# Turning convolved rows between two queries' products, keys ahead of broadcasts, and a bias add between left-over parts

## The chip, the core and the metric

The kernel runs on one core of a Trainium2 chip. The core has a matrix engine (TensorE, PE in the profile, with its weight loads as PEld), a vector engine (VectorE, DVE), an activation engine (ScalarE, ACT), GpSimd (POOL) and SyncE (SP), which issues most DMAs. Each engine works through its own list of instructions in order and they meet only through semaphores. The metric is the device time of one execution in microseconds.

## The reference

One tower block over 64 images of 2 x 104 x 104. Cut to what matters:

```python
concat = concatenate((x, left_up, right_up, left_down, right_down), axis=1)      # 10 channels
normed = (concat - mean) * rsqrt(var + 1e-7) * gamma + beta                      # per image
h = conv(normed, W, stride 8) + b                      # 169 tokens of 128 per image
xn = layernorm(h);  q, k, v = xn @ Wqkv.T              # 8 heads of 64
qp = exp(q * scale @ proj.T);  kp = exp(k @ proj.T)
D = qp @ kp.sum(tokens);  context = kp.T @ v
h = h + (qp @ context / (D + 1e-6)) @ Wout.T + bout
h = h + moe(layernorm(h))                              # 8 experts, the best 2, silu(x W) * (x V) @ W2
```

The attention is over all tokens of one image. The convolution's share that comes from `beta` is the same in all images; it is computed once as the map `cbeta`.

## The kernel before

The kernel has a token stage (to about 706 us of the trace) and an expert stage behind it. The change lies in the token stage.

The token stage goes over 32 pairs of images, in groups of four pairs (8 images). A step works on three pairs at once, as a pipeline: in step n, pair n is convolved and normalised (`a`), pair n-1 gets its queries, keys and context (`b`), pair n-2 its division by D and its attention output (`c`), and pair n-3 its routing (`d`). k is n modulo 4. While a group is worked on, the patches of the next group are made in seven front pieces: TensorE transposes a piece into bank 0 and VectorE multiplies it by gamma (L745). `TURN` says where: k = 1 and 2 have pieces at the places `front(2)` and `front(3)`, k = 3 at `front(0)`, `front(1)` and `front(2)`, k = 0 has none. The last group makes no pieces. In k = 1 VectorE also computes the image shift of the next group (L703, L707) right behind the bias add. Three steps more (n = 32 to 34) empty the pipeline.

The order on each engine is written out by hand in its `step`. The parts that the change and the prediction touch:

- TensorE: `q_feature(j)` (three matmuls of 362 columns, L627 to L629, into bank 4 or 5), for j = 0, 1 at the step's start; the sums D (L528); the convolution (L535, ten matmul instructions into bank 1); `q_feature(2)` and `(3)`; the transposes of the convolved rows h1 (L548, bank 2); `front(0)`; `broadcast(0)` and `(1)` (L498), which spread 1/D of two heads over the partitions, into banks 7 and 1 in turn; `k_tokens(0)` and `(1)` (three matmuls of 512 columns, L627 to L629, banks 4 and 5); `broadcast(2)`, `k_tokens(2)`, `broadcast(3)`; the first part of the context (L640); the transposes of the normalised rows (L633); `front(1)`; the products of queries and context (L581, bank 7); the rest of the context (L640, L646); `front(2)`; the transposes of the updated rows (L609); L653; `front(3)`.
- VectorE: 1/D (L812), whose value is split for TensorE's float32r input into a high part, four copies (L824), and a left-over part, four subtractions (L830), one for each of two images and two halves of their tokens; `rden_ready` is counted up behind the last. Then the bias add `h1 = conv + cbeta` (L837, two instructions), which waits for `conv_done` and releases `h1_ready`; statistics of the h1 transposes (L751, L754); `normalise(0)` and `(1)` (L794: the query features times a broadcast, each waits for its broadcast); in k = 3 the first front piece; `xtok` (L855), the normalised rows, which waits for `rstd` from GpSimd (L1128, L1130); `normalise(2)` and `(3)`; the choice of experts; and so on.
- ScalarE: the exponents of the four query products (L1066, L1067; `q_exp`) and of the three key products (L1083; `k_exp`), which also free banks 4 and 5.

## Time and profile before

| | |
|---|---|
| median of three runs | 1203.25 us (1201.57 to 1204.62) |
| the profiled execution's own time | 1201.72 us |
| its span, first to last instruction | 1199.9 us |
| granted TensorE clock, mean over the span | 0.968 of full speed |
| busy: PE, PEld | 1095.0 us (91%), 926.2 us (77%) |
| busy: DVE, ACT, POOL | 858.7 us (72%), 567.8 us (47%), 605.2 us (50%) |

Busy time is summed over the whole span and hides which wait ends last in a stage; matmuls are pipelined, so their recorded durations overlap and the distance from one start to the next says more. The steps themselves are very alike: between 95 and 645 us, the starts of two convolutions are 19.1 to 20.2 us apart, with the same spacing at every k. In the timeline, instructions of one line that follow each other closely are merged into one row (its start, its length, and xN).

### The profile page before, as it was taken

What the parts mean: (1) busy time and instruction counts of PE and PEld (TensorE: products, weight loads), DVE (VectorE), ACT (ScalarE), POOL (GpSimd) and SP (SyncE); (2) the same over time, 40 slices, a digit from 0 to 9 for tenths busy, and PEclk for the clock granted to TensorE, in tenths of its full rate; (3) what the DMA queues carried; (4) which work ended last, traced back from release to release, by engine and by line L of the source; (5) the groups of instructions that cost most, each with busy time, mean ns of one, the idle gap of its engine ahead of it and who ended that gap; (6) DMA issues with size and microseconds to landing.
All of it is one profiled execution on the core that took longest, in us unless ns stands there. A gap on an engine that the chain in (4) does not pass through costs nothing.

```text
span 1199.9 us, 30227 instructions
## 1 busy us (share of the span) xinstructions
PE 1095.0 (91%) x8632; PEld 926.2 (77%) x8633; DVE 858.7 (72%) x3327; ACT 567.8 (47%) x1318; POOL 605.2 (50%) x666
## 2 busy tenths in 40 slices
PE   2699999999999999999999726999999999999994
PEld 1567777777777777776766525999999999999994
DVE  4448787887787878878867584777777777777772
ACT  2343634535445354353333414555555555555551
POOL 2001535354445354444445452676666666666664
PEclk9799999999999999999999857999999999999997
DMA  9251131220301312101011143343444443444442
GB/s 155 49 140 60 34 73 33 47 60 27 80 26 36 72 34 63 44 30 33 27 33 32 34 119 63 54 55 53 55 53 54 56 55 53 54 54 53 57 54 21
DMA packets 75792, 65.54 MB, mean 55 GB/s; under 512 B 12382, under 2 KB 66718, under 8 KB 75712
## 3 DMA queue, kind: packets, MB, share of 16 engines
q0 software_dynamic: 33024, 25.86, 15.3%
q1 hardware_dynamic: 42496, 38.32, 13.7%
q8 instruction: 40, 0.66, 0.2%
q10 hardware_dynamic: 192, 0.37, 0.2%
q14 instruction: 40, 0.33, 0.1%
HBM read 32.81 MB, written 31.71 MB: 54 GB/s over the span
## 4 chain that ended last, share of the span: by engine, by line
PE 68%; issue 13%; DVE 7%; POOL 2%; SPq 1%; DMA 1%; ACT 1%; POOLq 0%; DVEq 0%; ACTq 0%
PE bank L1251 22%; PE bank L1263 13%; PE bank L581 7%; PE bank L653 4%; PE bank L640 3%; PE bank L646 3%; PE bank L535 3%; PE bank L627 2%; DVE patches L745 2%; DVE xtok L855 2%; PE bank L425 2%; DVE attn L794 2%; POOL rstd L1130 2%; PE bank L1239 2%; PE bank L628 2%
## 5 line engine op out<-in xcount | busy, mean ns | idle before, releaser
L1392 POOL DMA_INDIRECT out_rows<-yo,dest x184 | 302.2, 1643 | 168.8 <-issue 116.4
L1251 PE MATMUL bank<-xT_e,wv 128*128 128x256 f32 x2208 | 289.1, 286 | 1.0 <-DVE xT_e L1343 0.9
L1251 PEld LDWEIGHTS bank<-xT_e,wv 128*128 128x128 f32 x2208 | 271.9, 190 | 1.6 <-DVE xT_e L1343 1.3
L1155 POOL DMA_INDIRECT sorted_rows<-xrow_all,sloti x192 | 189.0, 984 | 74.7 <-issue 54.4
L1321 ACT ACTIVATE sil<-bank 128x256 f32<-128x256 f32 x368 | 141.5, 385 | 160.1 <-PE bank L1251 157.2
L1350 DVE TENSOR_TENSOR hid<-sil,bank 128x256 f32<-128x256 f32 x368 | 154.7, 421 | 84.2 <-ACT sil L1321 74.3
L1263 PE MATMUL bank<-w,hid 128*128 x1472 | 179.5, 275 | 1.0 <-DVE hid L1350 1.0
L1263 PEld LDWEIGHTS bank<-w,hid 128*128 128x128 f32 x1472 | 171.5, 192 | 1.2 <-issue 1.2
L1128 POOL TENSOR_SCALAR vare<-mv 128x3 f32<-128x3 f32 x64 | 12.5, 196 | 310.4 <-issue 255.0
L1306 ACT CAST wv<-wv_all 128x1024 fp32r x92 | 96.3, 1047 | 40.9 <-issue 27.9
L1066 ACT ACTIVATE attn<-bank 128x256 f32<-128x256 f32 x128 | 49.5, 387 | 131.1 <-PE bank L629 131.1
L535 PE MATMUL bank<-patches,wct 128*128 128x338 f32 x320 | 101.9, 467 | 2.3 <-DVE patches L745 2.3
L1333 DVE CAST wv<-wl_all 128x1024 fp32r x92 | 66.8, 726 | 37.2 <-issue 37.2
L745 DVE TENSOR_TENSOR patches<-bank,gam 128x416 f32<-128x416 f32 (+3 forms) x160 | 71.7, 502 | 29.4 <-PE bank L425 28.4
L581 PE MATMUL bank<-attn 128*128 128x169 f32 x512 | 83.2, 316 | 9.1 <-DVE attn L794 9.0
L581 PEld LDWEIGHTS bank<-attn 128*128 128x128 f32 x512 | 75.5, 193 | 16.2 <-DVE attn L794 16.2
L535 PEld LDWEIGHTS bank<-patches,wct 128*128 128x128 f32 x320 | 59.7, 194 | 31.4 <-issue 4.2
L1083 ACT ACTIVATE attn<-bank 128x512 f32<-128x512 f32 x96 | 57.3, 598 | 53.0 <-PE bank L629 51.8
L653 PE MATMUL bank<-wvo,attn 128*64 128x136 f32 x1024 | 75.9, 287 | 1.9 <-ACT attn L1107 1.0
L1107 ACT COPY attn<-bank 128x512 f32<-128x512 f32 x32 | 18.7, 586 | 111.0 <-PE bank L646 111.0
L1061 ACT COPY attn<-bank 128x272 f32<-128x272 f32 x128 | 50.0, 391 | 42.4 <-PE bank L653 39.4
L640 PE MATMUL bank<-attn,xtok 128*128 128x512 f32 x128 | 68.5, 617 | 0.0
(188 smaller groups left out, 1856.8 us busy)
## 6 DMA issues: line engine op xcount, KB each, us to landing
xr<-sorted_rows SPq DMA_DIRECT2D x92, 130.0 KB
raw<-in_x SPq DMA_DIRECT2D x64, 84.5 KB
raw<-in_x SPq DMA_DIRECT2D x60, 78.0 KB
out_rows<-attn SPq DMA_DIRECT2D x64, 58.5 KB
sorted_rows<-xrow_all,sloti POOLq DMA_INDIRECT x192, 2.3
out_rows<-yo,dest POOLq DMA_INDIRECT x184
wv_all<-in_L_ffn_W SPq DMA_DIRECT2D x8, 256.0 KB, 6.4
wv_all<-in_L_ffn_V SPq DMA_DIRECT2D x8, 256.0 KB, 6.7
```

What stands on the lines that cost most here:

```text
L535: t = pe.matmul(bank[1][:, 0:PT], wct[:, q], patches[:, par, q, 2 * k:2 * k + 2].rearrange("p b t -> p (b t)"), start=(q == 0), stop=(q == 4))
L581: t = pe.matmul(bank[7][:, TOK * i:TOK * i + TOK], mm[:, pc, i, j, 0:D], qf[:, pc, j, TOK * i:TOK * i + TOK], start=(j == 0), stop=(j == 3))
L640: pe.matmul(bank[(6, 1)[i]][:, :], xtok[:, p, i], kf[:, i], start=True, stop=False)
L653: t = pe.matmul(o_[64 * (h % 2):64 * (h % 2) + 64, col:col + D + HEADS], gT[:, i, NF * h:NF * h + NF], wvo[:, h], start=True, stop=True)
L745: t = ve.tensor_tensor(dst[:, lo:hi], src[:, i0:i0 + hi - lo, :, dy:dy + NP1], gam[:, q, lo:hi].unsqueeze(2).to_broadcast([128, hi - lo, G ...
L1155: po.indirect_dma_start(sorted_rows, bass.IndirectOffsetOnAxis(sloti[:, p, j, ch:ch + 1], 0), xrow[:, p, j, ch], None).then_inc(s(f"scatte ...
L1251: q = pe.matmul(bank[fc][:, TT * m:TT * m + TT], wv[:, p, w_, m, cols], xT[:, p, x_], start=(w_ + x_ == 0), stop=(w_ == 1))
L1263: q = pe.matmul(bank[4 + p][:, D * a:D * a + D], hid[:, p, fc, 128 * a:128 * a + 128], w2[:, bass.ds(e, 1), fc].rearrange("p e n -> p (e n ...
L1306: ac.copy(wv[:, p, 0].rearrange("p m n -> p (m n)"), wv_all[:, bass.ds(e, 1)].rearrange("p e m n -> p (e m n)")).then_inc(s("w_high"), 1)
L1321: ac.activation(sil[:, fc % 2], bank[fc][:, 0:TT], ACT.Silu).then_inc(s("silu_done"), 1)
L1350: ve.tensor_tensor(hid[:, p, fc], sil[:, fc % 2], bank[fc][:, TT:2 * TT], ALU.mult).then_inc(s("h_done"), 1)
L1392: po.indirect_dma_start(out, bass.IndirectOffsetOnAxis(dest[:, p, a:a + 1], 0), yo[:, p, a], None, compute_op=ALU.add).then_inc(s(f"added{ ...
```

## The change

On TensorE, the transposes of h1 move between `q_feature(2)` and `q_feature(3)`; and the order broadcast 0, broadcast 1, keys 0, keys 1, broadcast 2, keys 2, broadcast 3 becomes keys 0, broadcast 0, keys 1, broadcast 1, broadcast 2, keys 2, broadcast 3, with all of it behind `front(0)`. On VectorE, the four left-over subtractions are parted: two as before, then the bias add, then the other two; `rden_ready` is counted up twice a step, and TensorE waits for the second before broadcast 0. The work is the same, and the number of instructions too.

```diff
--- before.py
+++ after.py
@@ -537,9 +537,8 @@
                                       start=(q == 0), stop=(q == 4))
                     t.then_inc(s("conv_done"), 1)
                 if b:
-                    for j in range(2, 4):
-                        pe.wait_ge(s("q_exp"), 4 * mb + j - 1)
-                        q_feature(j)
+                    pe.wait_ge(s("q_exp"), 4 * mb + 1)
+                    q_feature(2)
                 if a:
                     pe.wait_ge(s("h1_ready"), n + 1)
                     at_least(pe, s("h2_copied"), n - 2)
@@ -547,24 +546,31 @@
                     for ch in range(NCH):
                         t = pe.transpose(bank[2][:, D * ch:D * ch + D], chunk(h1T[:, k], ch), ident)
                     t.then_inc(s("h1t_done"), 1)
+                if b:
+                    pe.wait_ge(s("q_exp"), 4 * mb + 2)
+                    q_feature(3)
                 front(0)
+                if b:
+                    pe.wait_ge(s("q_exp"), 4 * mb + 3)
+                    k_tokens(0)
                 if c:
-                    pe.wait_ge(s("rden_ready"), mc + 1)
+                    pe.wait_ge(s("rden_ready"), 2 * (mc + 1))
                     broadcast(0)
+                if b:
+                    pe.wait_ge(s("q_exp"), 4 * mb + 4)
+                    k_tokens(1)
+                if c:
                     if a:
                         pe.wait_ge(s("h1_ready"), n + 1)
                     broadcast(1)
+                    pe.wait_ge(s("qn_done"), 4 * mc + 1)
+                    broadcast(2)
                 if b:
-                    for j in range(2):
-                        pe.wait_ge(s("q_exp"), 4 * mb + 3 + j)
-                        k_tokens(j)
-                for j in range(2, 4):
-                    if c:
-                        pe.wait_ge(s("qn_done"), 4 * mc + j - 1)
-                        broadcast(j)
-                    if b and j < NCH:
-                        pe.wait_ge(s("k_exp"), NCH * mb + j - 1)
-                        k_tokens(j)
+                    pe.wait_ge(s("k_exp"), NCH * mb + 1)
+                    k_tokens(2)
+                if c:
+                    pe.wait_ge(s("qn_done"), 4 * mc + 2)
+                    broadcast(3)
                 if b:
                     pe.wait_ge(s("x_ones"), mb + 1)
                     pe.wait_ge(s("k_exp"), NCH * mb + 1)
@@ -819,17 +825,19 @@
                         at = 64 * u + 32 * i
                         return rden[at:at + 32, 0:(FIRST[1], PART)[u]]
 
+                    def low(u):
+                        for i in range(2):
+                            at = 64 - 64 * u + 32 * i
+                            t = ve.tensor_tensor(rparts[at:at + 32, i, FIRST[u]:(FIRST[1], TOK + 1)[u]], whole(u, i),
+                                                 high(u, i).bitcast(F32), ALU.subtract)
+                        t.then_inc(s("rden_ready"), 1)
+
                     for u in range(2):
                         for i in range(2):
                             t = ve.tensor_copy(high(u, i), whole(u, i))
                     t.then_inc(s("rden_high"), 1)
                     ve.wait_ge(s("rden_high"), mc + 1)
-                    for u in range(2):
-                        for i in range(2):
-                            at = 64 - 64 * u + 32 * i
-                            t = ve.tensor_tensor(rparts[at:at + 32, i, FIRST[u]:(FIRST[1], TOK + 1)[u]], whole(u, i),
-                                                 high(u, i).bitcast(F32), ALU.subtract)
-                    t.then_inc(s("rden_ready"), 1)
+                    low(0)
                 if a:
                     ve.wait_ge(s("conv_done"), n + 1)
                     at_least(ve, s("h2t_done"), n - 3)
@@ -837,6 +845,8 @@
                         t = ve.tensor_tensor(part(h1T[:, k]), by_image(bank[1][:, 0:PT])[:, :, tok],
                                              cbeta[:, tok].unsqueeze(1).to_broadcast([128, 2, tok.stop - tok.start]), ALU.add)
                     t.then_inc(s("h1_ready"), 1)
+                if c:
+                    low(1)
                 if fr and k == 1:
                     image_shift(g + 1)
                 if a:
```

## Rows read from the trace of the kernel before

**Rows 1.** The page, part 1: busy us (share of the span) and instructions.

```profile
PE 1095.0 (91%) x8632; PEld 926.2 (77%) x8633; DVE 858.7 (72%) x3327; ACT 567.8 (47%) x1318; POOL 605.2 (50%) x666
```

**Rows 2.** Windows of the steps k = 2, 3, 0, 1, cut at convolution starts.

```profile
core 0: us, PE busy (x) PEld busy (x) DVE busy (x) ACT busy (x) POOL busy (x), PEclk, DMA share, GB/s
...
332.11:351.65 19.54, 19.46 (x157) 14.68 (x152) 16.20 (x73) 7.25 (x20) 8.92 (x14) 1.00 0.10 30
...
370.91:390.80 19.89, 19.28 (x152) 14.23 (x148) 16.46 (x76) 10.74 (x23) 9.43 (x15) 1.00 0.10 32
sum 78.92, PE 77.03 PEld 56.99 DVE 63.15 ACT 36.36 POOL 36.62; mean PE 19.26 PEld 14.25 DVE 15.79 ACT 9.09 POOL 9.15
```

**Rows 3.** Timeline, TensorE, step k = 3: start us, us, engine, line, what.

```profile
335.55 0.33 PE L627 MATMUL bank<-xT,wqp 128*128 128x362 f32 x1
...
336.06 0.49 PE L548 MATMUL bank<-cst,h1T 128*128 128x128 f32 x3
336.38 0.52 PE L425 MATMUL bank<-cst,nrm 104*128 104x104 f32 x4
336.68 0.56 PE L498 MATMUL bank<-rparts,pick_head 104*128 104x340 f32 x2
337.08 0.40 PE L627 MATMUL bank<-wkp,xT 128*128 128x512 f32 x1
...
341.20 2.48 PE L581 MATMUL bank<-attn 128*128 128x169 f32 x16
```

**Rows 4.** Timeline, VectorE, the same step k = 3.

```profile
334.27 1.00 DVE L830 TENSOR_TENSOR rparts<-rden,rparts 32x84 fp32r<-32x84 f32 x4
335.30 0.57 DVE L837 TENSOR_TENSOR h1T<-bank,cbeta 128x256 f32<-128x256 f32 x2
...
337.38 0.32 DVE L754 BATCH_NORM_AGGREGATE mv<-bns 128x2 f32<-128x6 f32 x3
337.61 0.89 DVE L794 TENSOR_TENSOR attn<-attn,bank 128x338 f32<-128x338 f32 x2
338.42 0.58 DVE L745 TENSOR_TENSOR patches<-bank,gam 128x416 f32<-128x416 f32 x1
339.01 1.05 DVE L855 TENSOR_SCALAR xtok<-bank,mv,rstd 128x128 f32<-128x128 f32 x3
339.98 0.91 DVE L794 TENSOR_TENSOR attn<-attn,bank 128x338 f32<-128x338 f32 x2
```

**Rows 5.** Timeline, VectorE and then TensorE, step k = 2 from 390.80.

```profile
392.81 1.00 DVE L830 TENSOR_TENSOR rparts<-rden,rparts 32x84 fp32r<-32x84 f32 x4
393.94 0.57 DVE L837 TENSOR_TENSOR h1T<-bank,cbeta 128x256 f32<-128x256 f32 x2
...
397.70 1.05 DVE L855 TENSOR_SCALAR xtok<-bank,mv,rstd 128x128 f32<-128x128 f32 x3 [0.51 <-POOL rstd L1130]
...
398.83 0.52 PE L633 MATMUL bank<-cst,xtok 128*128 128x128 f32 x3
399.63 0.56 PE L581 MATMUL bank<-attn 128*128 128x169 f32 x2 [0.28 <-DVE attn L794]
```

**Rows 6.** Timeline, VectorE, step k = 1 from 370.91: image shift, statistics.

```profile
374.61 0.15 DVE L703 SCALAR_TENSOR_TENSOR imgshift<-imgstat,imgrstd 112x2 f32<-112x2 f32 x1
374.79 0.30 DVE L707 COPY nrm<-imgshift 112x64 f32<-112x64 f32 x2
375.38 0.69 DVE L751 BATCH_NORM_STATS2 bns<-bank 128x6 f32<-128x128 f32 x3 [0.29 <-PE bank L548]
```

**Rows 7.** Timeline, VectorE and then TensorE, step k = 0 from 351.65.

```profile
355.03 0.57 DVE L837 TENSOR_TENSOR h1T<-bank,cbeta 128x256 f32<-128x256 f32 x2
...
358.68 1.05 DVE L855 TENSOR_SCALAR xtok<-bank,mv,rstd 128x128 f32<-128x128 f32 x3 [0.51 <-POOL rstd L1130]
...
355.66 0.55 PE L548 MATMUL bank<-cst,h1T 128*128 128x128 f32 x3
```

**Rows 8.** Timeline, TensorE, the step past the last convolution.

```profile
668.92 0.94 PE L498 MATMUL bank<-rparts,pick_head 104*128 104x340 f32 x2 [3.31 <-DVE rparts L830]
669.66 0.63 PE L627 MATMUL bank<-wkp,xT 128*128 128x512 f32 x1
...
670.94 0.63 PE L627 MATMUL bank<-wkp,xT 128*128 128x512 f32 x1
```

## The prediction

> **What bounds the kernel now.** I read the page's busy times first, then the windows of the steps, then the timeline of TensorE and VectorE through one step of each kind. TensorE has work 91% of the span [rows 1]. The change lies only in the token stage, and there a group of four steps takes 78.9 us, with TensorE busy 77.0 of them and VectorE 63.2 [rows 2]. So TensorE bounds each step, less a small wait; what the reader should look for is where in a step TensorE waits, and for whom. I count from C, the start of a step's convolution; the windows are cut there. Steps go by their k: k = 3 holds the two early front pieces, k = 1 the image shift, k = 2 and k = 0 neither; the last four steps (no next group) look like k = 0.
>
> In k = 2, 1 and 0 TensorE stands still ahead of the context products (L581): 0.28 us by the record, 0.55 us in matmul starts (transposes from 398.83, three slots of 0.08, then nothing until 399.63), waiting for the fourth `normalise` on VectorE [rows 5]. The chain that ends there runs: convolution, bias add (L837), h1 transposes (L548), statistics (L751), `rstd` on GpSimd, `xtok` (L855), `normalise(2)` and `(3)` (L794), L581. In k = 3 there is no such wait: `normalise(3)` ends at 340.89 = C + 8.78 and L581 starts at 341.20 = C + 9.09, right behind front piece (1) [rows 3, 4]. VectorE has 0.31 us to spare there, and no more.
>
> **VectorE's part: the bias add between the left-over parts.** The four left-over subtractions take 1.00 us, so with two of them moved behind the bias add VectorE is free for the add 0.50 us earlier [rows 4]. But the add also waits for the convolution. In k = 2 the subtractions end at 392.81 + 1.00 = 393.81 and the add starts only at 393.94 = C + 3.14 [rows 5]; the 0.13 us gap is that wait. In k = 3 it starts at C + 3.19, right behind the subtractions [rows 4], in k = 0 at C + 3.38 [rows 7]. So after the change it starts at C + 3.14 in every step: earlier by 0, 0.05 and 0.24. It takes 0.57, and TensorE follows 0.06 later (355.03 to 355.66 in k = 0 [rows 7]). So the h1 transposes start at C + 3.77 at the earliest.
> The other two subtractions then run from C + 3.71 to 4.23, under the transposes, whose end (0.55 long [rows 7], and 0.04 to the next engine) lets the statistics start at C + 4.36: covered. In k = 1 they are not, since the image shift stands behind them. Before, it ran from 374.61 to 375.09, ahead of the statistics at 375.38 = C + 4.47 [rows 6]; now it ends at C + 4.23 + 0.48 = 4.71, and the statistics start 0.24 later than before.
>
> **TensorE's part 1: h1 transposes ahead of q3.** Before, q3's three matmuls (0.50 us) filled the wait for the bias add: in k = 3 q2 is through its slots at 335.55 = C + 3.44 and the transposes started at 336.06 = C + 3.95 [rows 3]. Now TensorE comes to the transposes at C + 3.44 and waits until C + 3.77: a new wait of 0.33 us in all 30 steps, while q3, ready, stands behind it. The transposes themselves gain 0.18 us (0.24 in k = 0).
> The Trainium skill says in "TensorE: Matmul & The Clock Gate", section "Architectural detail: the array is 16× 32×32, not 1× 128×128", that the engine's queue pulls weight loads ahead of running matmuls and leaves the matmuls in order. By this rule, the trace agrees: behind the last convolution the first broadcast waited 3.31 us while key products stood behind it [rows 8]. Could q3 slip past, k = 3 would lose 0.33 us less of TensorE's time and nothing of VectorE's, which binds there, so the sum would stay.
>
> **TensorE's part 2: keys ahead of broadcasts.** One k_tokens is three 512-column matmuls, 0.23 apart: 0.70. Before, both broadcasts stood ahead of the keys (336.68 to 337.08, 0.20 each) [rows 3] and `normalise(0)` at 337.61 = C + 5.50 had not to wait for them [rows 4]. The new order from C + 3.77: transposes 0.30, q3 0.58 (0.08 of it the change of operands), k0 0.70, broadcast(0) at C + 5.35, k1, broadcast(1) at C + 6.21. A broadcast is done 0.32 after its start and VectorE has it 0.04 later: `normalise(0)` from 5.71, `normalise(1)` from 6.57 to 6.97. VectorE works in order, so it comes to `xtok` at C + 6.97, whatever the statistics won. Against the row of each kind:
> - k = 2 (7 steps): `xtok` was at 397.70 = C + 6.90 [rows 5]: +0.07 each, +0.5.
> - k = 0 and the last group (10 steps): it was at 358.68 = C + 7.03 [rows 7]: -0.06 each, -0.6.
> - k = 1 (6 steps): the chain over the statistics binds: +0.24 each, +1.5.
> - k = 3 (7 steps): front piece (0), 0.30 on TensorE [rows 3], stands ahead of k0, so broadcast(1) starts at C + 6.51 and `normalise(1)` at 6.87. Behind it on VectorE stand the front piece's multiplication (338.42, 0.59 to the next) and only then `xtok` [rows 4]: 6.87 + 0.40 + 0.59 = C + 7.86, where it was 339.01 = C + 6.90, so 0.96 later. `normalise(3)` ends 1.88 behind, at 9.74, and L581 starts at C + 9.79 instead of 9.09: the spare time is used up, +0.70 each, +4.9.
>
> Behind L581 TensorE's work is the same and waits only for things that start from it, so these are whole losses or gains. TensorE's own queue would reach L581 by C + 8.6 in k = 2 (0.33 later than before), so the new wait costs nothing there: it comes out of the one ahead of L581.
> - The step past the last convolution: the first broadcast waits until 668.92, and k0 behind it takes from 669.66 to 670.94, 1.28 us at the wide spacing there [rows 8]. Now k0 runs inside that wait: -1.3, if ScalarE's last key exponent and what is queued behind it move up with it, else 0.
> - No issue of a DMA is moved, no queue is passed, and the expert stage is not touched.
>
> Sum: 0.5 - 0.6 + 1.5 + 4.9 - 1.3 = +5.0 us. On the profiled execution's own 1201.7 us that is 1206.7; the median of the runs shown is 1.5 above it, so I predict 1203.25 + 5.0 = 1208.3 us.
>
> **Bounds of the unknowns.** A change of operands may cost 0.08 more at k0 or k1: up to +0.1 in 30 steps, +3.0. In k = 1 VectorE overlaps neighbours by some hundredths: down to -0.6. In k = 3 the loss lies between 0.45 (steps on TensorE without any extra, `normalise` shorter) and 0.85: -1.7 to +1.1. The tail gives -1.3 or 0. From 1206.0 to, all at once, 1213.7; I take 1206 to 1212.5 as the forecast's own range.
>
> **Rivals.**
> 1. *Only k = 3 loses.* If broadcast(1) is out early enough, `xtok` follows `rstd` and keeps the transposes' gain: k = 0 -0.25 (10), k = 2 -0.17 (7), k = 1 +0.24 (6), k = 3 +0.70 (7), the tail: -2.5 - 1.2 + 1.5 + 4.9 - 1.3 = +1.4, 1204.7 us. For it: `normalise(1)` would have to end only 0.2 us earlier than I work out. Against: the matmuls that stand ahead of it have known spacings.
> 2. *Faster: the bias add doesn't wait for the convolution.* If it starts right behind two subtractions (C + 2.65 to 2.87), the transposes follow q2 at C + 3.44 without a wait and all of mine moves up 0.33: `xtok` at 6.64, so k = 0 -0.39 (10), k = 2 -0.26 (7), k = 1 -0.25 (6), k = 3 +0.37 (7), the tail: -3.9 - 1.8 - 1.5 + 2.6 - 1.3 = -5.9, 1197.4 us. It decides from an add start of about C + 2.9 down. Against it: the 0.13 us gap in k = 2, where VectorE was free [rows 5].
> 3. *TensorE's new wait is not given back.* 0.33 in the 23 steps of k = 0, 1 and 2 in place of my 1.4 there: 5.0 + 7.6 - 1.4 = +11.2, 1214.5 us. Against: the 0.55 us of slack ahead of L581.
> 4. *The waits merely move*, also in k = 3: 1203 us. Against: 0.31 us to spare there, and 0.96 wanted.
>
> **Chances.** Forecast 0.64, rival 1 0.13, rival 2 0.09, rival 3 0.07, rival 4 0.07. A difference under about 0.3% (3.6 us) can't be told from none. Of the forecast's share 0.03 may fall under it: slower 0.61 + 0.07 = 0.68, same 0.13 + 0.07 + 0.03 = 0.23, faster 0.09. The range 1202.5 to 1212.5 takes in the forecast and rivals 1 and 4, and leaves out 2 and 3.
>
> **What would show it.** The bias add at C + 3.14 and the h1 transposes at C + 3.77 in all steps, with TensorE idle from 3.44; `normalise(1)` released by its broadcast. In k = 3 `xtok` near C + 7.9, L581 near C + 9.8, TensorE waiting on L794; in k = 1 the statistics 0.24 later. A group of four steps, 78.9 long before, about 79.8 after (+0.07 - 0.06 + 0.24 + 0.70 = +0.95). I am wrong if the add starts before C + 3.0, if `normalise(1)` ends before C + 6.8, or if in k = 3 the front multiplication doesn't stand behind a late `normalise(1)`.

## The result, and the profile after

| | before | after |
|---|---|---|
| median | 1201.57 us (7 runs, 1201.09 to 1204.62) | 1207.06 us (7 runs, 1204.87 to 1208.58) |
| ratio, 95% interval | | 1.0042 [1.0031, 1.0053] |
| the profiled execution's own time | 1201.72 us | 1204.87 us |
| its span | 1199.9 us | 1203.1 us |
| mean granted clock | 0.968 | 0.972 |

The change makes the kernel 5.5 us slower, against a forecast of +5.0. Four more runs of before brought its median down from 1203.25 to 1201.57, so the forecast of 1208.3 lies 1.2 above the median of after. Ratios here are taken without the executions in a slower state of their chip (six of the 17 of before, and one of tail_keys, on one of the chips of the last section on experiments), so they are not the quotients of the medians.

Line numbers behind L540 move: the h1 transposes are L547 (L548 before), the query and key products L633 to L635, the transposes of the normalised rows L639, the products of queries and context L587 (L581), the left-over parts L831, the bias add L845 (L837), the statistics L757, `normalise` L800 (L794), the front piece's multiplication L751 (L745), `xtok` L865 (L855). For the experiments I name instructions by what they do, since each has lines of its own.

The page, part 1, of after, answers to [rows 1]. The work is the same (the same instruction counts on every engine), and TensorE's busy time too: the loss is waiting.

```profile
PE 1095.3 (91%) x8632; PEld 922.8 (77%) x8633; DVE 866.6 (72%) x3327; ACT 568.5 (47%) x1318; POOL 605.9 (50%) x666
```

The windows of the steps k = 2, 3, 0, 1 of after, cut at convolution starts, answer to [rows 2] (the third number from the end is the granted clock):

```profile
312.49:332.62 20.13, 19.23 (x151) 14.05 (x147) 16.39 (x75) 7.25 (x20) 8.94 (x14) 1.00 0.50 99
332.62:352.95 20.33, 19.91 (x155) 14.49 (x151) 16.49 (x73) 7.25 (x20) 8.94 (x14) 1.00 0.09 29
...
372.22:392.30 20.08, 19.34 (x151) 14.13 (x148) 16.58 (x76) 10.75 (x23) 9.43 (x15) 1.00 0.11 32
sum 79.81, PE 77.41 PEld 56.60 DVE 64.37 ACT 36.43 POOL 36.67; mean PE 19.35 PEld 14.15 DVE 16.09 ACT 9.11 POOL 9.17
```

A group takes 79.81 us where it took 78.92: +0.89, and k = 3 alone +0.79 (20.33 against 19.54). The clock is at its upper level in each window, so it has no part in this.

TensorE in step k = 3 (C = 332.62), from the timeline, answers to [rows 3]:

```profile
335.89 0.33 PE L635 MATMUL bank<-xT,wqp 128*128 128x362 f32 x1
336.40 0.55 PE L547 MATMUL bank<-cst,h1T 128*128 128x128 f32 x3 [0.17 <-DVE h1T L845]
336.70 0.41 PE L633 MATMUL bank<-xT,wqp 128*128 128x362 f32 x1
...
337.28 0.52 PE L425 MATMUL bank<-cst,nrm 104*128 104x104 f32 x4
337.58 0.48 PE L633 MATMUL bank<-wkp,xT 128*128 128x512 f32 x1
...
338.36 0.32 PE L498 MATMUL bank<-rparts,pick_head 104*128 104x340 f32 x1
...
339.22 0.49 PE L498 MATMUL bank<-rparts,pick_head 104*128 104x340 f32 x2
...
341.60 0.55 PE L639 MATMUL bank<-cst,xtok 128*128 128x128 f32 x3 [0.17 <-DVE xtok L865]
341.98 0.52 PE L425 MATMUL bank<-cst,nrm 104*128 104x104 f32 x4
342.43 1.84 PE L587 MATMUL bank<-attn 128*128 128x169 f32 x11
```

VectorE in the same step answers to [rows 4]:

```profile
334.78 0.49 DVE L831 TENSOR_TENSOR rparts<-rden,rparts 32x84 fp32r<-32x84 f32 x2
335.77 0.57 DVE L845 TENSOR_TENSOR h1T<-bank,cbeta 128x256 f32<-128x256 f32 x2 [0.50 <-PE bank L535]
336.37 0.49 DVE L831 TENSOR_TENSOR rparts<-rden,rparts 32x86 fp32r<-32x86 f32 x2
336.98 0.69 DVE L757 BATCH_NORM_STATS2 bns<-bank 128x6 f32<-128x128 f32 x3
...
338.73 0.51 DVE L800 TENSOR_TENSOR attn<-attn,bank 128x338 f32<-128x338 f32 x1 [0.64 <-PE bank L498]
339.58 0.51 DVE L800 TENSOR_TENSOR attn<-attn,bank 128x338 f32<-128x338 f32 x1 [0.35 <-PE bank L498]
340.00 0.58 DVE L751 TENSOR_TENSOR patches<-bank,gam 128x416 f32<-128x416 f32 x1
340.51 1.04 DVE L865 TENSOR_SCALAR xtok<-bank,mv,rstd 128x128 f32<-128x128 f32 x3
341.46 0.91 DVE L800 TENSOR_TENSOR attn<-attn,bank 128x338 f32<-128x338 f32 x2
```

The reader is to see three things. VectorE is ready for the bias add 0.50 us before the convolution is (the bracket behind L845 names L535). TensorE's transposes wait for the add (bracket behind L547), with q3 behind them, which was ready. And both `normalise` instructions, which used to stand back to back in one row [rows 4], are now two rows that each wait for their broadcast, L498. The front piece's multiplication and `xtok` follow the second without a gap, and L587 starts at 342.43 = C + 9.81, where it was C + 9.09. L587 has no bracket, though the prediction looked for one. It starts 0.06 behind the end of the last `normalise` (342.37) and 0.45 behind the front piece, where that distance was 0.36 before (340.84 to 341.20): the wait is 0.09 long, too short to be marked.

The table of waits of after sums this over the run (us in total, times, longest us):

```profile
DVE attn L800 <- PE bank L498: 20.8, 56, 0.7
DVE h1T L845 <- PE bank L535: 19.7, 32, 4.8
```

Before, the same table had 8.0 us in 2 waits for the second (the first steps, which fill the pipeline), and no row for the first.

### The profile page after: what moved, and what is told of

It is laid out like the page before. It is cut to its first block, busy times and chain, and to the rows that moved or that the text cites. A ratio compares the mean times of both kernels' runs of the same rounds, so it can differ in the third digit from the quotient of the medians.

```text
span 1203.1 us, 30227 instructions
## 1 busy us (share of the span) xinstructions
PE 1095.3 (91%) x8632; PEld 922.8 (77%) x8633; DVE 866.6 (72%) x3327; ACT 568.5 (47%) x1318; POOL 605.9 (50%) x666
## 4 chain that ended last, share of the span: by engine, by line
PE 75%; DVE 9%; issue 6%; SPq 2%; DMA 1%; ACT 1%; POOL 1%; POOLq 0%; DVEq 0%; ACTq 0%
PE bank L1261 22%; PE bank L1273 13%; PE bank L587 7%; PE bank L535 6%; PE bank L659 4%; PE bank L633 3%; PE bank L652 3%; DVE xtok L865 3%; DVE patches L751 2%; PE bank L646 2%; PE bank L634 2%; PE bank L635 2%; PE bank L425 2%; DVE attn L800 2%; PE bank L528 2%
## 5 line engine op out<-in xcount | busy, mean ns | idle before, releaser
L535 PE MATMUL bank<-patches,wct 128*128 128x338 f32 x320 | 99.9, 459 | 2.3 <-DVE patches L751 2.3
L587 PE MATMUL bank<-attn 128*128 128x169 f32 x512 | 85.7, 322 | 8.3 <-DVE attn L800 8.2
L751 DVE TENSOR_TENSOR patches<-bank,gam 128x416 f32<-128x416 f32 (+3 forms) x160 | 71.7, 502 | 27.6 <-PE bank L425 26.6
L587 PEld LDWEIGHTS bank<-attn 128*128 128x128 f32 x512 | 77.5, 197 | 15.8 <-DVE attn L800 15.0
L535 PEld LDWEIGHTS bank<-patches,wct 128*128 128x128 f32 x320 | 58.6, 191 | 30.6 <-issue 2.9
L800 DVE TENSOR_TENSOR attn<-attn,bank 128x338 f32<-128x338 f32 x128 | 61.5, 502 | 20.8 <-PE bank L498 20.8
```

The lines of the kernel that those rows point to most:

```text
L535: t = pe.matmul(bank[1][:, 0:PT], wct[:, q], patches[:, par, q, 2 * k:2 * k + 2].rearrange("p b t -> p (b t)"), start=(q == 0), stop=(q == 4))
L587: t = pe.matmul(bank[7][:, TOK * i:TOK * i + TOK], mm[:, pc, i, j, 0:D], qf[:, pc, j, TOK * i:TOK * i + TOK], start=(j == 0), stop=(j == 3))
L751: t = ve.tensor_tensor(dst[:, lo:hi], src[:, i0:i0 + hi - lo, :, dy:dy + NP1], gam[:, q, lo:hi].unsqueeze(2).to_broadcast([128, hi - lo, G ...
L800: ve.tensor_tensor(q, q, bank[(7, 1)[j % 2]][:, 0:PT + 2].rearrange("p (i t) -> p i t", i=2)[:, :, 0:TOK], ALU.mult).then_inc(s("qn_done"), 1)
```

## The experiments

The starts of two successive convolutions, median over the six or seven steps of one k between n = 2 and 27, tell where a kernel loses; the last three of the loop, which have no front piece, stand apart. "Loop" is from the convolution of n = 2 to that of n = 31. All from the profiled execution of each kernel, in us. In the column of ratios each is against before on the same chip.

| kernel | k = 0 | k = 1 | k = 2 | k = 3 | last three | loop | ratio [95%] |
|---|---|---|---|---|---|---|---|
| before | 19.26 | 19.89 | 19.95 | 19.54 | 19.15 | 568.80 | |
| the change | 19.27 | 20.09 | 20.06 | 20.33 | 19.11 | 575.82 | 1.0042 [1.0031, 1.0053] |
| split_only | 19.14 | 20.09 | 19.96 | 19.54 | 19.01 | 568.76 | 0.9992 [0.9982, 1.0002] |
| transposes_only | 19.27 | 19.83 | 19.85 | 19.97 | 19.15 | 571.03 | 1.0007 [0.9997, 1.0017] |
| keys_only | 19.27 | 19.89 | 19.97 | 19.95 | 19.14 | 571.85 | 1.0014 [1.0003, 1.0026] |
| k3_old_keys | 19.24 | 20.11 | 20.05 | 19.93 | 19.12 | 573.03 | 1.0015 [1.0005, 1.0025] |
| undo_keys_b | 19.04 | 20.10 | 19.85 | 19.95 | 18.90 | 570.09 | 1.0017 [1.0007, 1.0028] |
| tail_keys_b | 19.29 | 19.88 | 19.97 | 19.53 | 19.14 | 568.93 | 0.9991 [0.9982, 1.0] |
| chosen_b | 19.02 | 19.78 | 19.85 | 19.53 | 18.90 | 565.26 | 0.9967 [0.9954, 0.9979] |
| full_b | 19.26 | 20.10 | 20.07 | 20.34 | 19.11 | 575.93 | 1.0053 [1.0039, 1.0066] |

### The three parts alone

**split_only**: VectorE's part of the change, TensorE as before but for the count it waits for.

```diff
-                    pe.wait_ge(s("rden_ready"), mc + 1)
+                    pe.wait_ge(s("rden_ready"), 2 * (mc + 1))
...
+                    low(0)
                 if a:
                     ...                                        # the bias add
+                if c:
+                    low(1)
```

> The kernel before with VectorE's part alone: two left-over subtractions before the bias add, two behind it. My theory: the bias add starts at C + 3.15 in every step, but the h1 transposes still stand behind q3 and come at C + 3.94, so they gain only in k = 0 (0.07 us), VectorE's chain there 0.12 us in 10 steps: -1.2; in k = 1 the image shift delays the statistics by 0.2 in 6 steps: +1.3; k = 2 and 3 nothing. Sum 0 +- 1 us. Rival (the earlier bias add pays by itself): -3 us or more. Rival (VectorE's part carries the loss): +4 us.

Measured: 1200.77 us against 1201.8. The loop is unchanged, as two opposite terms: k = 0 and the last steps gain 0.12 to 0.14, k = 1 loses 0.20, where the image shift now runs later and holds up the statistics. By itself VectorE's part costs nothing over the loop.

**transposes_only**: q3 behind the transposes, all else as before (`first` is a switch that is on in every step here).

```diff
+                first = True
                 if b:
-                    for j in range(2, 4):
-                        pe.wait_ge(s("q_exp"), 4 * mb + j - 1)
-                        q_feature(j)
+                    pe.wait_ge(s("q_exp"), 4 * mb + 1)
+                    q_feature(2)
...
                 if a:
                     ...                                        # the transposes of h1
+                if b and first:
+                    pe.wait_ge(s("q_exp"), 4 * mb + 2)
+                    q_feature(3)
```

> The kernel before with the h1 transposes ahead of q3 and nothing else. My theory: TensorE waits at the transposes for the bias add (C + 3.82 to 4.01), 0.4 to 0.6 us, which comes out of the wait ahead of L581 in k = 0, 1, 2; the chain gains 0.11 (k = 2, 7 steps), 0.05 (k = 1, 6) and 0 (k = 0): -1.1. In k = 3, where that wait doesn't exist, TensorE is 0.4 us later: +2.8 in 7 steps. Sum +1.7 us. Rival (TensorE's new wait is lost in every step): 30 x 0.4 = +12 us. Rival (it is hidden in all steps): -1 us.

Measured: 1203.61 us against 1201.8; in the loop k = 3 loses 0.43, k = 1 and 2 gain 0.06 and 0.10. Two rows of TensorE's timeline in a step k = 3 of this kernel (C = 254.31) show why:

```profile
258.12 0.55 PE L551 MATMUL bank<-cst,h1T 128*128 128x128 f32 x3 [0.21 <-DVE h1T L843]
...
263.82 1.48 PE L587 MATMUL bank<-attn 128*128 128x169 f32 x9
```

The transposes wait until C + 3.81, 0.37 past the end of q2's slots, and the context products start at C + 9.51, 0.42 late. In k = 3 TensorE has no slack ahead of these products, so its wait is a loss there in full, with VectorE's order untouched. In the other steps the slack takes it.

**keys_only**: the new order of keys and broadcasts, all else as before.

```diff
                 front(0)
+                if b:
+                    pe.wait_ge(s("q_exp"), 4 * mb + 3)
+                    k_tokens(0)
                 if c:
                     pe.wait_ge(s("rden_ready"), mc + 1)
                     broadcast(0)
+                if b:
+                    pe.wait_ge(s("q_exp"), 4 * mb + 4)
+                    k_tokens(1)
+                if c:
                     if a:
                         pe.wait_ge(s("h1_ready"), n + 1)
                     broadcast(1)
...
```

> The kernel before with keys ahead of broadcasts and nothing else. My theory: broadcast(1) starts at C + 5.9 in k = 0, 1, 2, normalise(1) ends at C + 6.7, ahead of xtok at C + 6.9: nothing there. In k = 3 normalise(1) ends at C + 6.97, the front multiplication at 7.56, xtok 0.66 late, L581 0.40 late: +2.8 in 7 steps. In the step past the last convolution k0 runs inside the wait and the matmuls behind keep the full clock: -1.4. Sum +1.4 us. Rival (this part carries all of the loss): +5 to +6 us. Rival (the order doesn't matter but in the last step): -1.4 us.

Measured: 1203.61 us against 1201.8; k = 3 loses 0.41, the others nothing. VectorE's timeline in a step k = 3 of this kernel (C = 251.78):

```profile
257.49 0.51 DVE L798 TENSOR_TENSOR attn<-attn,bank 128x338 f32<-128x338 f32 x1
258.35 0.51 DVE L798 TENSOR_TENSOR attn<-attn,bank 128x338 f32<-128x338 f32 x1 [0.35 <-PE bank L498]
258.77 0.58 DVE L749 TENSOR_TENSOR patches<-bank,gam 128x416 f32<-128x416 f32 x1
259.28 1.04 DVE L859 TENSOR_SCALAR xtok<-bank,mv,rstd 128x128 f32<-128x128 f32 x3
```

Here only the second `normalise` waits. `xtok` starts at C + 7.50, 0.60 later than before, and the context products at C + 9.42, 0.33 later: 0.60 less the 0.31 to spare gives 0.29. The other 0.08 of the 0.41 are in the context products themselves, which take 2.56 us here and 2.48 before.

### The keys' order, with and without the others

**undo_keys_b**: the whole change but for the order of keys and broadcasts.

```diff
-                if b:
-                    pe.wait_ge(s("q_exp"), 4 * mb + 3)
-                    k_tokens(0)
                 if c:
                     pe.wait_ge(s("rden_ready"), 2 * (mc + 1))
                     broadcast(0)
-                if b:
-                    pe.wait_ge(s("q_exp"), 4 * mb + 4)
-                    k_tokens(1)
...
+                    for j in range(2):
+                        pe.wait_ge(s("q_exp"), 4 * mb + 3 + j)
+                        k_tokens(j)
```

> The whole change without keys ahead of broadcasts once more, since the chip of the first try took 1303 us for the kernel before. On a chip where that kernel takes 1201 to 1203 us, my theory gives +1.0 us: k = 0 -2.3, k = 2 -0.8, k = 1 +1.3, k = 3 +2.8. On a chip where it takes 1303 us: +20 us as before. Rival (these orders cost 1.5% on any chip): +18 us everywhere.

Measured: 1202.85 us against 1201.49; the loop is 1.3 longer than before's, where +1.0 was forecast. With the other two parts in place the keys' order thus costs 575.82 - 570.09 = 5.7 us in the loop, against 3.05 by itself. The rows of the table say where the difference comes from: k = 0, the last steps and k = 2 gain 0.22, 0.25 and 0.10 from the earlier bias add and transposes, and the late broadcasts take these back (by 0.23, 0.21 and 0.21); by itself the order found nothing to take there. In k = 3 it is 0.38 to 0.41 in both.

**k3_old_keys**: the whole change, with the old order of keys and broadcasts in k = 3 alone.

```diff
                 front(0)
+                if k != 3 or not a:
+                    ...                                        # keys 0, broadcast 0, keys 1, broadcast 1, ...
+                else:
+                    ...                                        # broadcast 0, 1, keys 0, 1, ...
```

> The whole change, but in k = 3 broadcasts and keys keep the old order. My theory: in k = 3 VectorE is on time (xtok at C + 6.8), TensorE is late by its wait at the transposes, L581 at C + 9.5 instead of 9.8: 0.3 to 0.4 us less in 7 steps, so +2.3 to +3.0 us against the kernel before, where the whole change has +5. Rival (the loss lies in all kinds of step alike): no more than 1 us less than the whole change.

Measured: 1203.78 us against 1201.8. k = 3 falls from 20.33 to 19.93 and the other kinds stay as in the whole change. `xtok` in k = 3 is back at C + 6.79, yet the context products start at C + 9.48: with VectorE early again, TensorE's own wait is next, 0.39 behind C + 9.09. So the loss in k = 3 has two layers, TensorE's wait and VectorE's chain, and the larger counts. With the old order of keys TensorE's layer ends at C + 9.48 to 9.51 (here and in transposes_only); front_first, below, shows how it stands with the new one.

**front_first**: the whole change, and on VectorE the front piece's multiplication ahead of the first two `normalise`.

```diff
                     norm_stats(lambda ch: bank[2][:, D * ch:D * ch + D], 0, n, s("ln1_bn"), s("ln1_mv"))
+                front(0)
                 if c:
                     ...                                        # normalise(0), normalise(1)
-                front(0)
```

> The whole change, and on VectorE front piece (0) of k = 3 stands ahead of normalise(0) instead of behind normalise(1). My theory: VectorE does the multiplication in its wait for broadcast(0), so normalise(1) ends at C + 7.3 as before and xtok follows at once, 0.55 earlier (C + 7.3 instead of 7.9); normalise(3) ends at 9.2, and L581 is then bound by TensorE at about C + 9.5 instead of 9.81. Against the whole change -0.3 in 7 steps, -2.2 us: +3 to +4 us against the kernel before, like the kernel with the old key order in k = 3. Rival (the loss of k = 3 is TensorE's alone, or comes from somewhere else): no change to the whole change, +5 to +6 us.

This one ran on a chip on which before takes 1306.07 us; it took 1314.55, 1.007 [1.0041, 1.0099], +8.5 where +3 to +4 was forecast. The whole change did not run on that chip, so the time does not tell what this edit gave. The chain in question can still be read: in k = 0, 1 and 2, where this kernel and the whole change have the same orders, the two profiles agree to 0.02 us from the bias add to the rank product behind the context products. VectorE's timeline in a step k = 3 of this kernel (C = 282.04):

```profile
287.43 0.56 DVE L751 TENSOR_TENSOR patches<-bank,gam 128x416 f32<-128x416 f32 x1
288.14 0.51 DVE L800 TENSOR_TENSOR attn<-attn,bank 128x338 f32<-128x338 f32 x1 [0.16 <-PE bank L498]
289.00 0.51 DVE L800 TENSOR_TENSOR attn<-attn,bank 128x338 f32<-128x338 f32 x1 [0.35 <-PE bank L498]
289.42 1.04 DVE L865 TENSOR_SCALAR xtok<-bank,mv,rstd 128x128 f32<-128x128 f32 x3
```

and TensorE's context products:

```profile
291.36 2.55 PE L587 MATMUL bank<-attn 128*128 128x169 f32 x16
```

The multiplication runs inside the wait for the broadcast. `normalise(0)` starts at C + 6.10, as in the whole change, `xtok` at C + 7.38 in place of 7.89, and the context products at C + 9.32 in place of 9.81. So of the loss of 0.72 ahead of them in k = 3, 0.49 is the multiplication that stands behind a late `normalise(1)`: the step of the prediction on which most of its sum rests. The forecast here had TensorE bind at about C + 9.5, as with the old order of keys. It does so at 9.32: the front piece (291.00) and the products stand at TensorE's own distance, 0.36, again, and the last `normalise` ends 0.07 earlier, so the two chains now arrive almost together. The new order of keys and broadcasts is itself shorter on TensorE, by 0.15 us (2.82 from the first instruction behind front piece (0) to the first context matmul, against 2.97 in k3_old_keys). So in the whole change TensorE alone would be 0.23 late in k = 3, and not 0.39 to 0.42.

### The step past the last convolution

**tail_keys_b**: before, with the new order of keys and broadcasts only where nothing is convolved any more.

```diff
                 front(0)
+                if not a:
+                    ...                                        # keys 0, broadcast 0, keys 1, broadcast 1, ...
+                else:
+                    ...                                        # as before
```

> The kernel before with keys ahead of broadcasts only in the step past the last convolution, once more. My theory: -1.4 us on any chip. Rival: 0.

Measured: 1200.86 us against 1201.49, 0.9991 [0.9982, 1.0]; the loop as before. From the last convolution to the sums D of the following step it takes 39.71 us, where before takes 41.05 and the whole change 39.51. So this corner of the change gains 1.3 to 1.5 in these traces; in the times it can hardly be told from nothing (the interval reaches 1.0). Over all kernels of this chip and the first pair, the stretch takes 38.25 to 39.71 us in the six with the new order there, and 40.36 to 41.25 in the four without: the gain is there each time, but its size goes with the granted clock of the single execution (see below, the tail).

### The parts that help

**chosen_b**: the split on VectorE (as in split_only); q3 behind the transposes except in k = 3; the new order of keys only past the last convolution; and, an edit that the change does not have, the image shift moved behind `normalise(1)`. Against before:

```diff
+                first = k != 3
                 if b:
                     ...                                        # q_feature(2)
+                if b and not first:
+                    pe.wait_ge(s("q_exp"), 4 * mb + 2)
+                    q_feature(3)
                 ...                                            # the transposes of h1
+                if b and first:
+                    pe.wait_ge(s("q_exp"), 4 * mb + 2)
+                    q_feature(3)
                 front(0)
+                if not a:
+                    ...                                        # keys 0, broadcast 0, keys 1, ...
...
-                if fr and k == 1:
-                    image_shift(g + 1)
+                if c:
+                    low(1)
...
                     normalise(1)
+                if fr and k == 1:
+                    image_shift(g + 1)
```

> The version put together from the theory, once more. On a chip where the kernel before takes 1201 to 1203 us: -5.2 us (k = 0 -2.3, k = 1 -0.7, k = 2 -0.8, tail -1.4). Where it takes 1303 us: +24 us as before. Rival (TensorE binds as soon as the wait ahead of L581 is shorter): -2 us. Rival (the orders cost nearly 2% on any chip): +22 us.

Measured: 1196.97 us against 1201.49, 0.9967 [0.9954, 0.9979]: faster than both kernels, by 4.5 and 10 us. Its slowest run (1198.1) is below the fastest of before's 22 (1199.1), and the loop agrees: -3.5, with -0.24, -0.11 and -0.10 in k = 0, 1, 2 and nothing in k = 3. Each kind of step gains what was forecast for it (0.23, 0.11, 0.11 and 0), and the 0.7 us between -4.5 and the -5.2 of the forecast lie within the interval. TensorE does become the bound, in k = 0, 1 and 2 alike, as the rival has it, but only at C + 8.74, 0.10 to 0.22 before the old start of the context products, so the gain is not cut short. In a step k = 1 (C = 288.29), first VectorE's timeline around the image shift:

```profile
292.65 0.69 DVE L780 BATCH_NORM_STATS2 bns<-bank 128x6 f32<-128x128 f32 x3
...
294.49 0.15 DVE L732 SCALAR_TENSOR_TENSOR imgshift<-imgstat,imgrstd 112x2 f32<-112x2 f32 x1
...
295.08 1.05 DVE L888 TENSOR_SCALAR xtok<-bank,mv,rstd 128x128 f32<-128x128 f32 x3
```

and TensorE's:

```profile
295.84 1.02 PE L669 MATMUL bank<-attn,xtok 128*128 128x512 f32 x2
296.70 0.49 PE L662 MATMUL bank<-cst,xtok 128*128 128x128 f32 x3
297.02 2.26 PE L610 MATMUL bank<-attn 128*128 128x169 f32 x14
```

The statistics are back at C + 4.36, `xtok` starts at C + 6.79, and the transposes of the normalised rows and the context products follow without a wait (no bracket): nothing that VectorE does earlier can help any more.

**full_b** is the whole change once more, beside the three above.

> The whole change as given, beside the three above. My theory: +5 us where the kernel before takes 1201 to 1203 us, as measured. Where it takes 1303 us I have no sum: the two kernels of the first try that share its VectorE part and its early h1 transposes were 1.5 and 1.9% slower there, so if those are the cause it is +20 us, and if the keys' place offsets them, less than +10.

Measured: 1207.85 us against 1201.49, 1.0053 [1.0039, 1.0066], with the steps of the first profile to 0.01 us.

### On another chip

undo_keys, tail_keys and chosen are the same kernels as those with the ending _b. They ran before those, on a chip on which before takes 1302.87 us.

> The whole change without keys ahead of broadcasts: the bias add between the left-over parts and the h1 transposes ahead of q3 stay. My theory: h1 transposes at C + 3.78 in all steps, xtok follows rstd at C + 6.79: k = 0 -0.23 (10 steps), k = 2 -0.11 (7), k = 1 +0.21 by the image shift (6), k = 3 +0.40 by TensorE's wait (7), tail 0: -2.3 - 0.8 + 1.3 + 2.8 = +1.0 us. Rival (the two parts help each other enough to pay): -3 us. Rival (TensorE's wait is lost everywhere): +8 us.

> The kernel before with keys ahead of broadcasts only in the step past the last convolution (n = 32). My theory: k0 runs inside the 3.3 us wait for the first broadcast, the granted clock stays at its upper level through the keys, and falls later, over L581: 3.1 us gained up to L581, 1.7 lost on it: -1.4 us. Rival (what is queued on ScalarE and VectorE doesn't move up): 0.

> A version put together from the theory: the left-over parts split in all steps; the h1 transposes ahead of q3 except in k = 3; the old order of broadcasts and keys except in the step past the last convolution; in k = 1 the image shift behind normalise(1). Expected: h1 transposes at C + 3.78 and xtok at C + 6.79 in k = 0, 1, 2: -0.23 (10), -0.11 (6), -0.11 (7); k = 3 unchanged; tail -1.4: -2.3 - 0.7 - 0.8 - 1.4 = -5.2 us, ratio 0.9957. Rival (TensorE binds as soon as the wait ahead of L581 is shorter): -2 us.

Measured: 1317.23, 1300.81 and 1322.48 us; ratios 1.0151 [1.0096, 1.0206], 1.001 [0.9972, 1.0048] and 1.0186 [1.0124, 1.0248]. The forecasts were +1.0, -1.4 and -5.2, so two of the three are far off: the version that wins 4.5 us on one chip loses 20 on the other. The argument about the first half of a step leaves out what costs time on this chip; the last part says what the traces show of it. It was the reason to run the three again.

## Why the prediction was right

**The bias add at C + 3.14.** It starts at 3.15 in every kind of step, with 0.29 (k = 0) to 0.64 (k = 2) of waiting for the convolution ahead of it. Rival 2 rested on its starting earlier; the 0.13 us gap of [rows 5] was the right row to read against it.

**The h1 transposes at C + 3.77.** Right: 3.77 to 3.78, in all steps. q3 does not slip past; its first matmul starts 0.30 behind the transposes. This is the rule of the Trainium skill ("TensorE: Matmul & The Clock Gate", section "Step-by-step: what each phase is for") that the matmuls themselves stay in program order, and the trace agrees, with q3 ready and held back 0.34 us (336.06 to 336.40).

**The broadcasts and `normalise(1)`.** Broadcast 0 at C + 5.74 in k = 3 (5.65 worked out), the first `normalise` at C + 5.71 in the other kinds (5.71). Rival 1 wanted `normalise(1)` to end 0.2 us earlier than I had it; it is rather later.

**`xtok`, kind by kind.**

| | predicted | measured | step, predicted | step, measured |
|---|---|---|---|---|
| k = 2 | C + 6.97 | 7.01 | +0.07 | +0.11 |
| k = 0 | C + 6.97 | 7.02 | -0.06 | +0.01 |
| k = 1 | +0.24 | +0.20 | +0.24 | +0.20 |
| k = 3 | C + 7.86 | 7.89 | +0.70 | +0.79 |

What was mis-sized are hundredths, seen in VectorE's timeline of a step k = 0 (C = 352.95):

```profile
359.54 0.51 DVE L800 TENSOR_TENSOR attn<-attn,bank 128x338 f32<-128x338 f32 x1 [0.37 <-PE bank L498]
359.97 1.04 DVE L865 TENSOR_SCALAR xtok<-bank,mv,rstd 128x128 f32<-128x128 f32 x3
```

`normalise(1)` starts at C + 6.59 (6.57 worked out) and has 0.43 to the next instruction. I took 0.40, half of the 0.81 of two that stand back to back [rows 4]. The 0.05 are nearly the whole gain of 0.06 that I gave to k = 0. In k = 3 another small term counts: the context products take 2.56 us when the last `normalise` ends just ahead of them, and 2.48 as they did before, when it had ended 0.31 us earlier [rows 3, 4], 0.08 that I had not counted.

**k = 3, the largest term.** +0.70 predicted, +0.79 measured, times 7. Its mechanism is shown from two sides: front_first takes the multiplication out of the chain and gets back 0.49 of 0.72 in the step, and what is left, 0.23, is TensorE's own lateness. k3_old_keys and transposes_only have 0.39 to 0.42 of it with the old order of keys. The prediction named both layers, and took the larger.

**The slack that hides TensorE's wait in k = 0, 1 and 2.** Right: transposes_only loses 0.01 in k = 0, and gains 0.06 and 0.10 in k = 1 and 2. Rival 3 is refuted by it; rival 4 by k = 3.

**The tail.** -1.3 predicted, -1.54 measured, but by another road. Windows of before around its broadcasts and keys, and then around the context products:

```profile
668.90:674.10 5.20, 5.18 (x14) 4.32 (x15) 0.92 (x2) 1.27 (x3) 1.91 (x5) 0.50 0.08 26
677.30:680.00 2.70, 2.66 (x20) 2.67 (x20) 2.46 (x14) 0.00 (x0) 0.00 (x0) 1.00 0.00 0
```

and of after around the same instructions:

```profile
673.00:675.20 2.20, 2.12 (x10) 1.72 (x11) 1.04 (x3) 0.60 (x1) 1.92 (x5) 1.00 0.18 61
678.50:682.80 4.30, 4.22 (x19) 4.22 (x19) 3.29 (x19) 0.00 (x0) 0.00 (x0) 0.60 0.00 0
```

The third number from the end is the granted clock. Before, TensorE stood 3.31 us still [rows 8], and its clock was at the lower level for all of the keys and broadcasts that followed. After, k0 runs in the middle of the wait, the longest standstill is 2.06 us (timeline of TensorE, below), and the keys behind it run at the upper level, 0.23 apart. By the context products 3.1 us were gained (29.02 from the last convolution, against 32.14). Then these products, behind a wait of 2.33, took 4.24 us at 0.60 of the clock, where they had taken 2.56 at full clock, which gave back 1.7.

```profile
673.08 0.42 PE L498 MATMUL bank<-rparts,pick_head 104*128 104x340 f32 x1 [2.06 <-DVE rparts L831]
...
678.58 4.24 PE L587 MATMUL bank<-attn 128*128 128x169 f32 x16 [2.33 <-DVE attn L800]
```

So the net of the term came out by luck: I had counted only k0's own 1.28, where the runs show 3.1 gained and 1.7 lost over the granted clock. tail_keys_b repeats the net (-1.34) with the same two parts. But the broken wait does not always keep the clock: in keys_only k0 runs inside the same wait, the longest standstill is 2.22, and the broadcasts and keys behind it run at 0.50 all the same.

```profile
669.60:672.40 2.80, 2.74 (x8) 2.38 (x9) 1.00 (x3) 0.60 (x1) 1.91 (x5) 0.50 0.14 48
```

**The sum.** Loop +7.0 (predicted +0.5 - 0.6 + 1.5 + 4.9 = +6.3), tail -1.5, together +5.5, as are the medians: 1207.06 - 1201.57 = 5.5. The profiled executions lie only 3.2 apart, because that of after is 2.7 ahead before the loop is in its rhythm. Its first convolution took 3.08 us, at a granted clock of 1.00, where before's took 4.77 at 0.64. keys_only, k3_old_keys, chosen_b and full_b have 3.08 too, split_only, transposes_only, undo_keys_b and tail_keys_b 4.77. The order of instructions need have no part in it: one kernel has both (chosen 4.77, the same kernel as chosen_b 3.08, behind the same standstill of 2.27 us). The profiles with 3.08 have a mean clock of 0.972 or 0.973 and those with 4.77 0.968 or 0.969, and among the unprofiled executions on the first experiments' chip before has both values as well. So the medians, and not the two profiles, are the ones to compare.

## What to carry to other kernels

Where an instruction is moved ahead of another engine's input, work out when that input arrives and follow it on the receiving engine up to the first instruction that had no slack: here a second broadcast that came 1.8 us later (C + 6.60 in place of 4.77) made most of the loss in one kind of step of four, and the busy share of TensorE did not move. Parts of a change that each cost little alone can take back each other's gains (3.05 us alone, 5.7 beside the others), so cost them together, by kind of step. And where steps differ, make the change where its row says that it helps: the edits placed by kind, with the image shift moved out of the way, gave -4.5 us in place of +5.5. That holds on the chips on which before takes 1201 us; on another the same kernel loses 20.

## What the runs showed of the hardware

**A short run of work inside a long wait kept the clock up in four kernels of six.** In before, 3.31 us of standstill were followed by 5.2 us at 0.50. With the wait broken by one key product (2.03 to 2.27 us of standstill) the whole change, full_b, tail_keys_b and chosen_b ran on at 1.00, and the lower level came later, behind another wait of 2.33. In keys_only (2.22) it was there when the wait ended, and in k3_old_keys (2.24) it came 1.6 us after. In the four kernels with the unbroken wait (3.30 to 3.35) it was there at the end of the wait in two, before and split_only, and came 0.4 and 1.4 us after it in transposes_only and undo_keys_b. Each is a single profiled execution.

**A run of matmuls is a little longer when its input comes just in time.** The 16 context products take 2.48 us where the last `normalise` ended 0.31 us or more ahead of them (k = 3 of before, transposes_only, k3_old_keys), and 2.54 to 2.56 where it ends less than 0.1 ahead, with a recorded wait (before, k = 0) or without one (chosen_b, k = 0; front_first, k = 3): the same instructions at the same granted clock.

**The same program takes 1201 us on one chip and 1303 and 1306 us on two others.** In steps k = 0, 1 and 2 of front_first, which ran on one of the two, the first half is that of the whole change to 0.02 us. Its loop takes 673.19 us where the whole change takes 575.82 on the first chip, 3.4 us more a step. The table of waits of front_first names (us in total, times, longest us):

```profile
ACT attn L1117 <- remote: 93.7, 20, 6.8
DVE slots L943 <- remote: 77.7, 27, 3.9
...
PE bank L615 <- DVE h1T L888: 62.3, 29, 3.2
```

Before, on the first chip, has no wait marked remote among its hundred longest, and 1.7 us in one wait in place of the last row. "Remote" says only that the profile found nobody whose work ended where the wait did. The kernel says more: `slots` waits for `rank_done`, which is counted up by nothing but TensorE's rank product (L593 before, L599 here). In before `slots` starts 0.04 us behind the recorded end of that product:

```profile
363.15 0.38 PE L593 MATMUL bank<-both,cst 128*128 128x24 f32 x2
363.57 0.18 DVE L933 TENSOR_TENSOR slots<-bank,cst 128x24 f32<-128x24 f32 x1 [0.18 <-PE bank L593]
```

and in front_first, in one step, 3.36 behind it (293.89 + 0.38 = 294.27):

```profile
293.89 0.38 PE L599 MATMUL bank<-both,cst 128*128 128x24 f32 x2
297.63 0.18 DVE L943 TENSOR_TENSOR slots<-bank,cst 128x24 f32<-128x24 f32 x1 [2.99 <-remote]
299.16 1.73 PE L615 MATMUL bank<-ident_gate,h1T 128*128 128x136 f32 x6 [2.35 <-DVE h1T L888]
```

So on these chips VectorE gets TensorE's own result late, in nearly every step, the updated rows come late, TensorE stands still for them, and the 4.5 us behind that wait run at a granted clock of 0.50 (mean over the loop 0.924, against 1.00 on the first chip). Over the loop the profiles have this lateness, as a mean of 28 steps, at 2.67 us in tail_keys, 2.82 in front_first, 3.07 in undo_keys and 3.37 in chosen (0.09 to 0.11 in before, the whole change and chosen_b on the first chip), with loops of 665.1, 673.2, 672.0 and 682.3 us. The longer the lateness, the higher the kernel's ratio to before (1.001, 1.007, 1.0151, 1.0186); each is a single profiled execution, and no run changes the lateness alone. Why the result comes late there, and by a different amount in each kernel, stays open.
